# Preparing a graph-attention layer beside the last strips of an attention layer: other engines compare and normalise, and one score row travels through DRAM

## The chip, the cores and the metric

The kernel runs on one core of a Trainium2 chip. The metric is the device time in microseconds of one execution; three runs of the kernel before gave 799.28, 801.04 and 801.62 us, median 801.04 us. The trace is from a further, profiled execution.

## The reference, cut to what matters

```python
def ref(x, adj, Wq, bq, Wk, bk, Wv, bv, W, a):        # x: 4096 x 128, adj: 4096 x 4096
    h = max(layernorm(x), 0)
    q, k, v = h @ Wq.T + bq, h @ Wk.T + bk, h @ Wv.T + bv
    s = where(adj > 0, q @ k.T / sqrt(128), NEG)
    x = x + elu(softmax(s) @ v)                         # first layer
    h = max(layernorm(x), 0)
    hw = h @ W
    s1, s2 = hw @ a[:128], hw @ a[128:]
    e = where(adj > 0, leaky_relu(s1[:, None] + s2[None, :], 0.01), NEG)
    return x + hw + softmax(e, axis=1) @ h              # second layer
```

In the second layer exp(leaky_relu(s1+s2)) takes one of two products of a row factor and a column factor, by the sign of s1+s2. So the kernel needs one bit for each pair (i, j), the sign of s1[i]+s2[j], cut with the mask bit, and two matmuls of such fp8 bit matrices with weighted rows of h.

## The kernel before, in words

A strip is 128 rows of the 4096; T = 32 strips, NC = 8 chunks (also called groups) of four. The program has three blocks, and a block ends when every engine has finished its part of it.

Block 1 (up to about 40 us) normalises x and makes q, k and v. Block 2 is the first layer, one period for each strip: TensorE makes scores (L998 to L1000), VectorE adds the mask (L811), ScalarE takes the exponential (L691), the weights are turned (L1009, L1025, DMA transposes L549) and multiplied with v (L1044, L1045), and GpSimd (POOL) prepares mask bytes (L592) and masks (L607) and the ELU (L623 to L626), with VectorE's batch-norm statistics (L846) of the new x behind it. Each engine's order is written out by hand in a function `period`, and `all_periods` runs it.

Beside and behind the last strips block 2 prepares the second layer, chunk by chunk. VectorE's `variance` and `inverse_root` (L856 to L874) give the mean and 1/std; GpSimd's `normalise` (L635) subtracts and scales chunks 0 to 6, VectorE (L954) chunk 7; TensorE's `turn_h` (L1098) turns a chunk, ScalarE's `hT_out` (L767) copies it out; `s_products` (L1105, L1109) makes the s1 and s2 columns, and the s1 row spread over all partitions by a matmul with `wa_rep`; ScalarE's `s_out_of` (L773 to L777) copies both out; VectorE's `weigh` (L883) makes weighted h, GpSimd's `split_words` (L644) cuts it in a high and a low half; `hw_product` (L1114) and `add_hw` (L327) add hW. The signs of the first group's four strips are made for 32 key tiles: strips 0 and 1 (EARLY) in block 2, for each chunk two tiles on ScalarE (`sign_bytes`, L297), one on VectorE and one on GpSimd (`compare_bytes`, L302). At its end VectorE finds the maxima over all rows (L963 to L983, with TensorE L1133 to L1136) and cuts strip 0's bits (L312, L316, L321).

On the SyncE (SP) queue stand, after the last three transposes of block 2's own low parts (L549), eight DMA transposes (`load_mask`, L308) which bring the mask words of groups 0 and 1.

Block 3 is the second layer. For strips 2 and 3 of group 0 (LATE) the signs are still to be made: VectorE does ten tiles, GpSimd 22 (`VECTOR_LATE = 10`). `cut(0, 0, 2)` waits until both are done. TensorE runs 64 matmuls (L1466) for each strip, waiting for `parts_ready` of that strip and for `sums_out` of the strip two before. ScalarE makes the signs of group g+1 while TensorE runs group g: 11, 11 and 10 tiles of all four strips, each lot followed by `copy_sums` (L1401) of one strip, and the group's `signs_ready` after the third lot. `cut` of group g+1 waits for it. SP stores results and loads masks of group g+2.

## Time and profile before

| what | value |
|---|---|
| median of three runs | 801.04 us (799.28 to 801.62) |
| the profiled execution's own time | 802.26 us |
| its span, first to last instruction | 800.5 us |
| TensorE busy | 731.8 us, 91% of the span |
| VectorE, ScalarE, GpSimd busy | 572.9, 547.7, 481.9 us |
| mean granted TensorE clock | 0.963 of 2.4 GHz |

The span splits in three: block 1 to about 40 us, block 2 to about 547 us, block 3 to the end. In a timeline row stand the start in us from the span's start, the time in us, engine, line, operation, tiles out<-in with their shape and the count merged in the row; in brackets is how long the engine sat idle before and what released it. An "SPq" row is the time that the queue's sequencer took to issue. GpSimd (POOL) shares with VectorE (DVE) the way to the on-chip memory, so the same instruction is seen with more than one duration.

### The profile page before, as it was taken

What the parts mean: (1) busy time and instruction counts of PE and PEld (TensorE: products, weight loads), DVE (VectorE), ACT (ScalarE), POOL (GpSimd) and SP (SyncE); (2) the same over time, 40 slices, a digit from 0 to 9 for tenths busy, and PEclk for the clock granted to TensorE, in tenths of its full rate; (3) what the DMA queues carried; (4) which work ended last, traced back from release to release, by engine and by line L of the source; (5) the groups of instructions that cost most, each with busy time, mean ns of one, the idle gap of its engine ahead of it and who ended that gap; (6) DMA issues with size and microseconds to landing.
All of it is one profiled execution on the core that took longest, in us unless ns stands there. A gap on an engine that the chain in (4) does not pass through costs nothing. (4 is left out here: it accounts for less than half of the span.)

```text
span 800.5 us, 18318 instructions
## 1 busy us (share of the span) xinstructions
PE 731.8 (91%) x6229; PEld 613.4 (77%) x6229; DVE 572.9 (72%) x1219; ACT 547.7 (68%) x1082; POOL 481.9 (60%) x375
## 2 busy tenths in 40 slices
PE   4975999999999999999999998649299999999996
PEld 2554888888888888888888877438288888888885
DVE  4847687878787878787878894597294775685572
ACT  5944678787878787878787866445548977977910
POOL 1068499999999999999999969997700000000000
PEclk9987999999999999999999999688699999999999
DMA  6059999999898988888988646700043434334100
GB/s 223 1 187 246 271 212 264 251 264 255 254 257 255 255 256 256 254 256 255 255 255 255 198 94 108 157 0 1 1 106 73 90 70 86 86 84 88 36 10 12
DMA packets 189323, 130.86 MB, mean 163 GB/s; under 512 B 170336, under 2 KB 176992, under 8 KB 181088
## 3 DMA queue, kind: packets, MB, share of 16 engines
q1 hardware_dynamic: 188544, 130.05, 60.4%
q8 instruction: 24, 0.39, 0.2%
q10 hardware_dynamic: 576, 0.26, 0.1%
q14 instruction: 19, 0.16, 0.1%
q0 software_dynamic: 160, 0.00, 0.0%
HBM read 69.47 MB, written 18.87 MB: 110 GB/s over the span
## 5 line engine op out<-in xcount | busy, mean ns | idle before, releaser
L811 DVE CUSTOM_DVE_ANT_0 scores<-ps_s,mask_both 128x1024 f32<-128x1024 f32 x128 | 155.7, 1217 | 27.9 <-POOL mask_both L607 17.5
L592 POOL TENSOR_SCALAR mask_bytes<-adj_both 128x2048 uint8<-128x2048 int32 x64 | 146.2, 2301 | 44.8 <-POOLq L80 40.0
L691 ACT ACTIVATE scores<-scores,neg_max 128x1024 f32<-128x1024 f32 x128 | 146.0, 1142 | 24.8 <-DVE neg_max L817 24.8
L830 DVE TENSOR_TENSOR low<-scores 128x1024 bf16<-128x1024 f32 x96 | 137.5, 1432 | 27.0 <-ACT scores L691 22.5
L607 POOL TENSOR_SCALAR mask_both<-mask_bytes 128x2048 bf16<-128x2048 uint8 x64 | 151.4, 2365 | 5.4 <-POOL mask_bytes L592 0.4
L1044 PE MATMUL spare<-v_parts,hiT 128*128 128x256 bf16 x768 | 141.5, 274 | 8.0 <-DMA lowT<-low 7.3
L705 ACT ACTIVATE hiT<-spare 128x512 bf16<-128x512 bf16 (+1 forms) x128 | 103.0, 805 | 58.2 <-PE spare L1025 55.6
L1045 PE MATMUL spare<-v_parts,lowT 128*128 128x128 bf16 x768 | 134.7, 220 | 0.0
L1466 PE MATMUL ps_x<-q_parts,over_k 128*128 128x258 bf16 x1024 | 117.0, 275 | 15.4 <-DVE over_k L321 14.0
L1466 PEld LDWEIGHTS ps_x<-q_parts,over_k 128*128 128x128 fp8e4 x1024 | 99.5, 98 | 31.1 <-DVE over_k L321 14.3
L998 PE MATMUL ps_s<-k_hi,q_strip 128*128 128x512 f32 x256 | 113.9, 445 | 6.6 <-DVE row_max L811 4.3
L1000 PE MATMUL ps_s<-k_hi,q_strip 128*128 128x512 f32 x256 | 102.7, 401 | 0.0
L999 PE MATMUL ps_s<-k_lo,q_strip 128*128 128x512 f32 x256 | 102.0, 399 | 0.0
L1044 PEld LDWEIGHTS spare<-v_parts,hiT 128*128 128x128 bf16 x768 | 75.5, 98 | 16.5 <-issue 8.0
L297 ACT ACTIVATE v_parts<-s_block,s_col 128x512 fp8e4<-128x512 f32 x128 | 79.6, 716 | 0.0
L1401 ACT ACTIVATE sums<-ps_x,ac 128x258 f32<-128x258 f32 x64 | 26.5, 466 | 77.6 <-PE ps_x L1466 77.6
L1045 PEld LDWEIGHTS spare<-v_parts,lowT 128*128 128x128 bf16 x768 | 75.5, 98 | 0.7
L823 DVE TENSOR_TENSOR pT_low<-spare,pT_high 128x512 bf16<-128x512 f32 x64 | 44.0, 687 | 29.6 <-ACT pT_high L698 29.5
L1025 PE MATMUL spare<-ident_half,scores 128*128 128x128 bf16 x768 | 64.8, 220 | 0.0
L1025 PEld LDWEIGHTS spare<-ident_half,scores 128*128 128x128 bf16 x768 | 44.9, 98 | 25.5 <-issue 25.1
L698 ACT ACTIVATE pT_high<-spare 128x512 bf16<-128x512 f32 x64 | 37.7, 590 | 38.4 <-PE spare L1009 37.5
L998 PEld LDWEIGHTS ps_s<-k_hi,q_strip 128*128 128x128 f32 x256 | 49.4, 193 | 15.4 <-DVE row_max L811 5.1
(154 smaller groups left out, 1346.1 us busy)
## 6 DMA issues: line engine op xcount, KB each, us to landing
adj_both<-in_adj SPq DMA_DIRECT2D x64, 1024.0 KB, 5.3
mask_bytes_dram<-mask_bytes SPq DMA_DIRECT2D x32, 512.0 KB, 2.8
x_sb<-in_x SPq DMA_DIRECT2D x8, 256.0 KB, 7.8
out<-res SPq DMA_DIRECT2D x32, 64.0 KB, 1.5
lowT<-low SPq DMA_TRANSPOSE x96, 4.7
over_k<-mask_bytes_dram SPq DMA_TRANSPOSE x16, 4.5
scores<-mask_bytes_dram SPq DMA_TRANSPOSE x16, 4.6
raw_w<-in_L_gnn_Wq ACTq DMA_DIRECT2D x1, 64.0 KB, 3.1
```

The lines of the kernel that those rows point to most:

```text
L592: nc.gpsimd.tensor_scalar(mask_bytes[b % 2][:, half(h)], adj_sb[h], 1.0, 0.0, ALU.min, ALU.max).then_inc(bytes_ready, 1)
L607: nc.gpsimd.tensor_scalar(out, src, -NEG, NEG, ALU.mult, ALU.add).then_inc(mask_ready, 1)
L691: nc.scalar.activation(sc, sc, ACT.Exp, bias=neg_max[:, bn:bn + 1], accum_out=row_sum[:, bn, k:k + 1]).then_inc(exp_done, 1)
L705: nc.scalar.activation(hiT[k][:, half_of], ps_t[(2 + u) % 3][:].bitcast(BF16)[:, half_of], ACT.Copy).then_inc(hiT_ready, 1)
L811: nc.vector.tensor_tensor_reduce(out=scores[bn % 2][:, part(k)], in0=ps_s[k % 2][:], in1=mask[bn % 2][:, part(k)], scale=1.0, scalar=LOWES ...
L830: nc.vector.tensor_tensor(low[k][:], p, high_half(p), ALU.subtract).then_inc(low_done, 1)
L998: nc.tensor.matmul(o, high, k_hi[:, col], start=True, stop=False)
L1000: last = nc.tensor.matmul(o, rest, k_hi[:, col], start=False, stop=True)
L1025: last = nc.tensor.transpose(out[:, D * t:D * t + D], high[:, D * t:D * t + D], ident_half[:])
L1044: nc.tensor.matmul(ps_a[:], high, v_parts[:, t, :, :], start=(i == 0 and n == 0), stop=False)
L1045: last = nc.tensor.matmul(ps_a[:, 0, :], rest, v_parts[:, t, 0, :], start=False, stop=(i == NC - 1 and n == 3))
L1466: last = nc.tensor.matmul(ps_x[b % 2][k][:], by_key_tile(m, t)[:, b], v1[k][:, t, :].bitcast(BF16), start=(t == 0), stop=(t == T - 1))
```

## The change

- GpSimd's `normalise` and VectorE's use `(x + minus_mean) * rstd` in place of `(x - mean) * rstd`; VectorE makes `minus_mean`.
- VectorE normalises chunks 0 and 1 (at the start of its last period) and 7, GpSimd chunks 2 to 6. Statistics of chunks 0 to 6 are worked out in one go in the period of strip T-2, not in two lots in those of T-4 and T-2 (with the root of the first in T-3).
- GpSimd makes no sign bytes. Per chunk ScalarE makes three early tiles, VectorE one. Of the late ones VectorE makes 16, ScalarE 16 at its start of block 3, and ScalarE's lots for group 1 become 0, 16 and 16.
- The s1 row isn't made by TensorE and copied out by ScalarE; SP writes the s1 column of a chunk to DRAM (element by element) and reads it back spread over 128 partitions, in three pieces (chunk 0; 1 to 3; 4 to 7), behind the eight mask transposes in its queue.
- The order on TensorE, ScalarE, VectorE and GpSimd behind the last period is written anew: the ELU of the last strip comes before chunks 2 and 3 are copied out, all `hw_product` come before the maxima are turned, `cut(0, 0, 2)` comes before `add_last_hw`.

```diff
@@ sync, behind the last period
                     for b in range(4):
                         load_mask(sp, 1, b, 1)
+                    for i, cs in enumerate(S1_CHUNKS):          # 0:1, 1:4, 4:8
+                        sp.wait_ge(s_out, cs.stop)
+                        for c in range(cs.start, cs.stop):
+                            sp.dma_start(s1_dram[c].rearrange("t p -> p t"), s_col[:, 4 * c:4 * c + 4, 0],
+                                         allow_slow_non_contiguous=True).then_inc(s1_stored[i], 16)
+                        sp.wait_ge(s1_stored[i], 16 * (cs.stop - cs.start))
+                        row = s1_dram[cs.start:cs.stop].rearrange("c t p -> (c t p)")
+                        sp.dma_start(s1_row[:, 512 * cs.start:512 * cs.stop], row.partition_broadcast(D)).then_inc(s1_in[i], 16)
@@ gpsimd
-                            last = nc.gpsimd.tensor_scalar(h_sb[:, t, :], x_sb[:, t, :], stats["moments"][:, t, 0:1],
-                                                           stats["rstd"][:, t:t + 1], ALU.subtract, ALU.mult)
+                            last = nc.gpsimd.tensor_scalar(h_sb[:, t, :], x_sb[:, t, :], minus_mean[:, t:t + 1],
+                                                           stats["rstd"][:, t:t + 1], ALU.add, ALU.mult)
...
-                            for n in range(6):
+                            for n in range(BY_VECTOR, BY_VECTOR + 2):
                                 normalise(n)
                     all_periods(pool, period)
+                    normalise(5)
+                    add_elu(T - 2)
+                    normalise(6)
+                    add_halves(T - 1)
                     split_words(0)
-                    add_elu(T - 2)
-                    split_words(1)
-                    add_halves(T - 1)
-                    split_words(2)
                     add_elu(T - 1)
-                    for c in range(3):
-                        early_sign(c)
-                    for c in range(3, NC):
-                        early_sign(c)
+                    for c in range(1, NC):
                         split_words(c)
@@ scalar
-                        act.wait_ge(s1_made, c + 1)
-                        nc.scalar.activation(s1_row[:, 512 * c:512 * c + 512], ps_s1, ACT.Copy).then_inc(s1_out, 1)
                     def early_signs(c):
                         act.wait_ge(s_out, c + 1)
-                        act.wait_ge(s1_out, 1)
-                        for t in (4 * c, 4 * c + 1):
+                        act.wait_ge(s1_in[0], 16)
+                        for t in range(4 * c, 4 * c + 3):
...
+                    s_out_of(0)
+                    acc_copy(T - 1, 3)
+                    s_out_of(1)
+                    elu_exp(T - 1)
                     hT_out(2)
                     hT_out(3)
+                    for c in range(2, NC - 2):
                         s_out_of(c)
                         early_signs(c - 2)
+                        if c + 2 < NC - 1:
+                            hT_out(c + 2)
@@ vector
+                        if not ahead:
+                            for n in range(BY_VECTOR):
+                                normalise(n)
                         turned_low(s, 0)
                         low_part(s, b, 1)
...
                     weigh(0)
-                    early_sign(0)
-                    weigh(1)
-                    early_sign(1)
                     dve.wait_ge(epi_done, T - 1)
                     moments_of(T - 2)
-                    weigh(2)
-                    early_sign(2)
-                    weigh(3)
+                    aggregate(slice(T - 4, T - 1))
+                    weigh(1)
+                    early_sign(0)                     # waits for s1_in[0]
                     dve.wait_ge(epi_done, T)
                     moments_of(T - 1)
-                    variance(slice(28, 32))
+                    aggregate(slice(T - 1, T))
+                    add_eps(slice(28, 32))
                     inverse_root(slice(28, 32))
+                    normalise(NC - 1)
+                    early_sign(1)
+                    for c in range(2, NC - 1):
                         weigh(c)
                         early_sign(c)
-                        add_hw(c - 4)
+                        if c >= 3:
+                            add_hw(c - 3)
@@ block 3
-                VECTOR_LATE = 10
+                VECTOR_LATE = 16
-                @block.gpsimd
-                def _(pool):
-                    for t in range(VECTOR_LATE, T):
-                        last = compare_bytes(nc.gpsimd, 0, s1_row, t, LATE)
-                    last.then_inc(late_signs, 1)
@@ vector
-                        last.then_inc(late_signs, 1)
+                        last.then_inc(vector_late, 1)
+                        cut(0, 0, 2)
                         add_last_hw(dve)
-                        for b in range(2, 4):
-                            cut(0, 0, b)
+                        cut(0, 0, 3)
@@ scalar
+                        for t in range(VECTOR_LATE, T):
+                            last = sign_bytes(0, s1_row, t, LATE)
+                        last.then_inc(late_signs, 1)
...
-                                    for t in range(11 * b, min(11 * b + 11, T)):
-                                        last = sign_bytes(1 - par, s1_block[:], t)
+                                    first_group = isinstance(g, int) and g == 0
+                                    for t in (range(16 * b - 16, 16 * b) if first_group else range(11 * b, 11 * b + 11)):
+                                        if 0 <= t < T:
+                                            last = sign_bytes(1 - par, s1_block[:], t)
```

## Rows read from the trace of the kernel before

**Rows 1.** The chain that ended last, its last part: start us, us, what.
```profile
786.80 7.19 PE ps_x L1466 x64
```

**Rows 2.** The timeline of TensorE before and at the start of block 3.
```profile
529.88 1.10 PE L1109 MATMUL ps_s<-scores,wa_rep 128*128 128x512 f32 x2
...
540.91 6.29 PE L1114 MATMUL spare<-w_next,scores 128*128 128x128 f32 x32
548.56 14.47 PE L1466 MATMUL ps_x<-q_parts,over_k 128*128 128x258 bf16 x128 [1.36 <-issue]
577.07 15.97 PE L1466 MATMUL ps_x<-q_parts,over_k 128*128 128x258 bf16 x128 [14.03 <-DVE over_k L321]
```

**Rows 3.** The timeline of VectorE in block 3.
```profile
552.70 4.02 DVE L302 TENSOR_SCALAR over_k<-mask_both,s_col 128x256 uint8<-128x256 f32 x10
574.53 1.23 DVE L316 SCALAR_TENSOR_TENSOR over_k<-over_k 128x1024 uint32<-128x1024 uint32 x1 [14.82 <-POOL over_k L302]
```

**Rows 4.** By stretch: length, busy PE, PEld, DVE, ACT, POOL; granted clock; DMA.
```profile
532.00:534.00 2.00, 0.00 (x0) 0.00 (x0) 2.00 (x3) 2.00 (x6) 2.00 (x2) 0.61 0.00 0
580.00:582.00 2.00, 2.00 (x19) 1.69 (x17) 1.83 (x9) 0.00 (x0) 0.00 (x0) 0.95 0.00 0
```

**Rows 5.** The timeline of ScalarE, end of block 2 and start of block 3.
```profile
531.51 2.49 ACT L297 ACTIVATE over_k<-mask_both,s_col 128x256 fp8e4<-128x256 f32 x6
549.83 0.63 ACT L1409 ACTIVATE s_block<-mask_both 128x512 f32<-128x512 f32 x1
557.34 0.82 ACT L1401 ACTIVATE sums<-ps_x,ac 128x258 f32<-128x258 f32 x2
558.05 6.84 ACT L297 ACTIVATE v_parts<-s_block,s_col 128x512 fp8e4<-128x512 f32 x11
```

**Rows 6.** The waits of TensorE from 440 to 486 us.
```profile
PE spare L1044 <- DVE pT_low L823: 1.6, 1, 1.6
```

**Rows 7.** The timeline of VectorE beside the last strips and at block 2's end.
```profile
490.24 1.21 DVE L830 TENSOR_TENSOR low<-scores 128x1024 bf16<-128x1024 f32 x1
518.36 0.29 DVE L846 BATCH_NORM_STATS2 bn<-x_sb 128x6 f32<-128x128 f32 x1 [0.35 <-POOL x_sb L626]
519.94 0.17 DVE L868 TENSOR_SCALAR seed<-moments 128x4 int32<-128x4 int32 x1
522.38 2.59 DVE L954 TENSOR_SCALAR adj_both<-x_sb,moments,rstd 128x128 f32<-128x128 f32 x4
534.88 0.15 DVE L963 TENSOR_REDUCE hT_total<-hT_sum 128x1 f32<-128x8 f32 x1
543.38 0.68 DVE L327 TENSOR_TENSOR x_sb<-x_sb,spare 128x512 f32<-128x512 f32 x1
```

**Rows 8.** Single lines and tiles: ns min/median/max, first and last start.
```profile
L954 DVE TENSOR_SCALAR adj_both<-x_sb,moments,rstd x4: 340/786/1084, 522.4 to 523.9; 128x128 f32<-128x128 f32 x4
L302 DVE TENSOR_SCALAR over_k<-mask_both,s_col x18: 343/518/594, 502.8 to 556.2; 128x256 uint8<-128x256 f32 x18
L635 POOL TENSOR_SCALAR adj_both<-x_sb,moments,rstd x28: 785/787/1745, 478.1 to 504.3; 128x128 f32<-128x128 f32 x28
```

**Rows 9.** The timeline of the SP queue behind the last strip.
```profile
492.96 10.03 SPq L308 DMA_TRANSPOSE over_k<-mask_bytes_dram  x4
503.11 10.06 SPq L308 DMA_TRANSPOSE scores<-mask_bytes_dram  x4
```

**Rows 10.** DMA issues of the page, and of the first 25 us: KB, us to landing.
```profile
adj_both<-in_adj SPq DMA_DIRECT2D x64, 1024.0 KB, 5.3
out<-res SPq DMA_DIRECT2D x32, 64.0 KB, 1.5
...
scores<-mask_bytes_dram SPq DMA_TRANSPOSE x16, 4.6
...
a_cols<-in_L_gnn_a POOLq DMA_DIRECT2D x2, 0.5 KB, 7.0
```

**Rows 11.** Groups of instructions by line, 485 to 548 us: busy us, mean ns.
```profile
L883 DVE SCALAR_TENSOR_TENSOR q_parts<-adj_both,q_parts 128x512 f32<-128x512 f32 x16 | 16.3, 1060 | 7.0 <-ACT s_col L775 7.0
```

More of the change, by code:

```diff
@@ L285, in build @@
             sem("signs_ready"), sem("mask_scaled"), sem("lower_part_ready"), sem("mask_cut"))
-        late_signs, hw_made = sem("late_signs"), sem("hw_made")
+        late_signs, vector_late, hw_made = sem("late_signs"), sem("vector_late_signs"), sem("hw_made")
+        s1_in = [sem(f"s1_rows_in{i}") for i in range(3)]
         def by_key_tile(m, t, dt=FP8):
@@ L497, in build @@
                 turned_x = [ps_s[0][:, 512 * i:512 * i + 512] for i in range(2)]
-                ps_s2, ps_s1 = ps_s[1][:, 0:512], ps_s[1][:, 512:1024]
+                ps_s3 = [ps_s[1][:, 512 * i:512 * i + 512] for i in range(2)]
+                ps_s2 = ps_s3[0]
                 block = c2.enter_context(nc.Block())
@@ L848, in _, with aggregate, add_eps @@
                     tail = Steps(dve, tail_own)
+                    def aggregate(cs):
+                        dve.wait_ge(bn_done, cs.stop)
+                        for t in range(cs.start, cs.stop):
+                            tail.mark(nc.vector.bn_aggr(stats["moments"][:, t, :], stats["bn"][:, t, :]))
+                    def add_eps(cs):
+                        mean, var = stats["moments"][:, cs, 0], stats["moments"][:, cs, 1]
+                        tail.wait()
+                        tail.mark(nc.vector.tensor_scalar(minus_mean[:, cs], mean, -1.0, None, ALU.mult))
+                        tail.do(nc.vector.tensor_scalar(var, var, EPS, None, ALU.add))
                     def variance(cs):
-                        bn, moments, spread = stats["bn"][:, cs], stats["moments"][:, cs], newton[:, 0, cs]
+                        bn, moments, spread = stats["bn"][:, cs], stats["moments"][:, cs], newton[:, cs]
                         mean_e, mean_o, m2_e, m2_o = (bn[:, :, i] for i in (1, 4, 2, 5))
@@ L860, in variance @@
                                                                  in1=stats["root"][:, cs], op0=ALU.mult, op1=ALU.mult))
-                        tail.mark(nc.vector.tensor_scalar(mean, mean, 0.5, None, ALU.mult))
+                        tail.mark(nc.vector.tensor_scalar(minus_mean[:, cs], mean, -0.5, None, ALU.mult))
                         tail.do(nc.vector.tensor_scalar(var, var, 1.0 / D, EPS, ALU.mult, ALU.add))
@@ L876, in inverse_root, with normalise @@
                             tail.do(ins)
+                    def normalise(c):
+                        for t in range(4 * c, 4 * c + 4):
+                            last = nc.vector.tensor_scalar(h_sb[:, t, :], x_sb[:, t, :], minus_mean[:, t:t + 1],
+                                                           stats["rstd"][:, t:t + 1], ALU.add, ALU.mult)
+                        last.then_inc(h_by_vector, 1)
                     def weigh(c):
@@ L985, in _ @@
                     cut_upper(0, 0).then_inc(parts_ready, 1)
-                    add_hw(3)
                 @block.tensor
@@ L1077, in period @@
                             make_scores(s + 2, b % 2, 0)
-                        if not ahead:
-                            s_products(0)
                         turn_high(s, b, 2)
@@ L1084, in period @@
                             make_scores(s + 2, b % 2, 1)
-                        if not ahead:
-                            turn_h(2)
                         turn_high(s, b, 3)
@@ L1121, in _ @@
                     s_products(1)
+                    turn_h(2)
                     turn_h(3)
@@ L1136, in _ @@
                     nc.tensor.matmul(ps_s2[:, 0:2], ones[0:2, :], top_diag[:], start=True, stop=True).then_inc(top_b, 1)
-                    for c in range(4, NC):
-                        hw_product(c)
         if True:
@@ L1332, in general @@
                         add_last_hw(dve)
+                        for rows in s1_in:
+                            dve.wait_ge(rows, 16)
                         dve.wait_ge(g_high, 1)
@@ L1405, in body @@
                             if more:
+                                if isinstance(g, int) and g < 2:
+                                    act.wait_ge(s1_in[g + 1], 16 * 1)
                                 act.wait_ge(signs_ready, g + 1)
```

98 lines of the change are left out of this document (42 added, 56 removed).

## The prediction, made before the changed kernel was run

> **What bounds the kernel now.** I read the chain that ended last first, backwards from the end. It is TensorE's L1466 without a break, 64 matmuls and 7.18 us for each strip, up to 793.99 us, and then 6.5 us of copying, adding and storing to 800.5 [rows 1]. So in block 3 only what delays TensorE counts. The timeline of TensorE shows the one hole: strips 0 and 1 run from 548.56 to 563.03 us, strip 2 starts at 577.07, after 14.03 us of waiting [rows 2]. VectorE's timeline says for whom: its cut of strip 2 waits 14.82 us for GpSimd's compare L302, and starts 0.04 us after the last of 22 compares has ended at 574.49; cutting takes 574.53 to 577.07, 2.54 us [rows 3]. Behind the hole the granted clock is 0.5, that is 1.2 GHz, for some 3 us before it returns to 2.4 GHz [rows 4]; strips 2 and 3 take 15.81 us (577.07 to 592.88) where 14.36 are due, so the hole costs 1.45 us more. Before block 3, TensorE ends block 2 with 32 matmuls at the low clock, to 547.20, and the block change takes 1.36 us [rows 2]. I call the start of strip 0 T0, 548.56 before. Then the old end is T0 + 251.9.
>
> **Block 3 after the change.** VectorE's ten late compares took 4.02 us; 16 take 6.4 [rows 3]. From T0 + 4.1 (552.70) they end at T0 + 10.6, scale and cut of strip 2 (0.6 + 2.54) at T0 + 13.75, before strips 0 and 1 are done at T0 + 14.5. ScalarE's 16 late signs at 0.415 us (2.49 / 6) [rows 5] take 6.6 us from T0 + 1.3 to T0 + 7.9: hidden under VectorE's. So GpSimd's 14.03 us go. What is late next is ScalarE, which has taken over work and given up none. Its row copy and gate take 0.77 (549.83 to 550.60), a lot of eleven signs 6.73 from its start to the next copy (so 0.612 each) and the copy of one strip's sums 0.71 (557.34 to 558.05) [rows 5]. T0 + 7.9 + 0.77 + 0.71 + 16 x 0.612 + 0.71 + 16 x 0.612 = T0 + 29.7; only then are group 1's signs ready, VectorE cuts for 2.54 and strip 4 can start at T0 + 32.2. Strips 0 to 3 are done at T0 + 28.9, or T0 + 30.3 if strip 0 meets the low clock: a hole of 1.9 to 3.3 us takes the place of 14. The clock paid at T0 hides in it. The other 28 strips take 28 x 7.18 = 201.0, the tail 6.5: the end is T0 + 239.8, and block 3 gives 12.1 us. `add_last_hw` is moved behind the cut, 2.5 us before strip 3's cut, which is needed only at T0 + 21.7: free. For later groups ScalarE needs 32 x 0.612 + 4 x 0.71 + 0.77 = 23.2 us against 28.7 of TensorE: it catches up in group 2.
>
> **T0 after the change.** Three things move it.
>
> First, statistics. TensorE waits 1.6 us for VectorE once between 440 and 486 us [rows 6], beside the first statistics lot; that lot leaves, so all behind comes 1.6 us earlier. It returns in the period of T-2 as one lot 28 wide, with ops hardly longer than those 4 wide: nothing more.
>
> Second, VectorE's last period has eight `normalise` instructions ahead of its low parts. Four such took 2.59 us beside a busy GpSimd; the shortest single one took 0.34 us [rows 7, 8], and 0.27 apart is my estimate from it. So 2.2 to 5.2 us (GpSimd normalises at the same time, which speaks for the upper end). The last low part, done at 491.45 before [rows 7], is then done at 491 to 494. On it hang the last own transpose and, in one queue, the eight mask transposes, which are issued from 492.96 to 513.17 [rows 9]. They now end at 512.8 to 515.7; I take 514.3.
>
> Third, the row. Chunk 0's store stands behind them all, though its s1 column is made near 499. VectorE's `early_sign(0)` waits for it, and behind that wait stand the last strip's statistics, `normalise` of chunk 7, six `weigh` and the maxima; ScalarE's `early_signs(0)` waits too, with every later copy behind it. No row shows this store. The transposes before it land 2.1 us after their issue has ended (4.6 less 2.5), a 64 KB store lands in 1.5 us; the column loads of 128 single elements took 7.0 us from another, busy queue [rows 10]. The store has 512 elements: from 1.5 to 4 x 7.0 = 28 us. I take 2.8, since the 64 KB store is of the same queue and the column loads sat among the x loads. The read back of 256 KB lies between 1.5 (64 KB) and 5.3 (1 MB) [rows 10]; I take 2.4. With 0.2 for the waits the row is there 5.4 us after the queue is free: X = 519.7. [...]
>
> VectorE from X to the end of block 2, each between uncontended and contended with GpSimd: eight early compares 0.27 to 0.5 each; last statistics, about 0.9 ahead of a root of 2.44 (519.94 to 522.38); four `normalise` 1.1 to 2.6; six `weigh` (two instructions of 1.06 each on the mean, 16.3 for all eight) 1.3 to 2.1; four `add_hw` 0.6; maxima, turning, cuts 534.88 to 543.4, of which its own `weigh` and compare are counted already, some 5 to 6 [rows 7, 8, 11]. Sum 22 to 31. GpSimd now has only eight splits there and no compares, so I take 27.3. TensorE and ScalarE are done before: ScalarE's signs need about X + 16. With 1.35 for the block change T0 = 519.7 + 27.3 + 1.35 = 548.4, where it was 548.56. What leaves VectorE's path there (waiting for GpSimd's chain, which ended at 518.3 and now ends near 509) is eaten by the wait for the row; five early pieces of VectorE's work now stand behind it. TensorE's last 32 matmuls (6.29 us) go from the end to where it waits anyway: that is 3.1 us (547.20 against VectorE's 544.06) which the longer VectorE chain fills.
>
> **The sum.** 548.4 + 239.8 = 788.2 us of span against 800.5, 12.3 us less. The profiled execution took 802.26 us, 1.2 above the median of the runs; the median should fall by the same 12.3 to 788.7. GpSimd's `add` in place of `subtract` I count at nothing: its 20 `normalise` take at most 0.79 us each, 15.8 together [rows 8], from the statistics at about 483.5; with some 8 us of ELU, halves and one split the last ELU is done near 508 to 509, 10 us before X. Cheaper ones lengthen only that pause.
>
> **Rivals.**
> A, the forecast: the row at about 520, strip 4 late by ScalarE; 788.7. Chance 0.45.
> B, the lower bounds hold: VectorE is little disturbed and its work from X takes 23, T0 = 544; 784. For it, GpSimd drops 30 compares; against it, each `weigh` is followed at once by a split. Chance 0.18.
> C, the transfer is slower: 10 us from queue to row, T0 = 553, and the hole before strip 4 lets the clock fall (1.45 us); 795. After TensorE's instructions ended at 530.98 us the stretch from 532 to 534 has 0.61, so it fell near 532.4, 1.5 us into the pause [rows 2, 4]. Chance 0.21.
> D, slower than before: the store goes element by element at the price of the column loads, 28 us. Then X = 545, T0 = 574, the end 814. It decides from a round trip of 17.5 us (X = 532, T0 = 560.7). Against it, the low bound is a row of this very queue. Chance 0.09. The Trainium skill, DMA: Bandwidth & Descriptors, Rules for kernel authors, speaks against this change: a plain DMA with rearranged access is given as 19 times slower than the hardware transpose; 19 times 1.5 us would be that rival's 28 us. No row here shows it.
> E, no change: a round trip of 13 to 18 us, T0 near 560, gives back what block 3 gains; 801. Chance 0.07. That GpSimd's work merely moves, with ScalarE as late as GpSimd was, would need signs twice as long as measured; it is in this chance.
>
> **How the numbers follow.** The forecast is A, 789. Within 0.3% (2.4 us, about what this kernel's measurement can tell from no change) lies E; faster A, B and C, 0.84; slower D, 0.09. The range leaves out D, E and the edges of B: 782 to 798.
>
> **What would show it.** Right: no `L302` on GpSimd; no wait of VectorE for GpSimd in block 3; strip 4's matmuls preceded by 2 to 3 us of idle with ScalarE's signs before the cut; VectorE idle from about 504 to 520 before an L302 with a DMA as its releaser; the SP queue's mask transposes ended near 514 and the row 5 us later; strips at 7.18 us. Wrong: T0 beyond 553 or below 544; a hole before strip 2; VectorE's first idle put down to GpSimd; TensorE or ScalarE, not VectorE, ending block 2.

## The result and the profile after

The changed kernel takes 796.45 us, median of seven runs (794.48 to 798.74), beside 801.54 us for the kernel before in runs taken with them (799.28 to 803.25). The ratio is 0.9939, 95% interval 0.9919 to 0.9960: 5.1 us less, where 12.3 were forecast. The profiled execution took 797.06 us, its span is 795.3 us, 5.2 less than before.

| | before | forecast | after |
|---|---|---|---|
| row of chunk 0 in place (X) | | 519.7 | 524.8 |
| start of strip 0 (T0) | 548.56 | 548.4 | 553.95 |
| strip 2 starts | T0 + 28.5 | T0 + 14.5 | no hole |
| strip 4 starts | | T0 + 32.2 | T0 + 33.7 |
| end of the span | T0 + 251.9 | T0 + 239.8 | T0 + 241.35 |

The SP queue of the changed kernel, timeline (start us, us to issue, line, operation); it answers [rows 9]:

```profile
501.63 9.15 SPq L311 DMA_TRANSPOSE scores<-mask_bytes_dram  x4
510.83 0.58 SPq L587 DMA_DIRECT2D s_row_dram<-s_col  x1
521.25 0.33 SPq L591 DMA_DIRECT2D mask_both<-s_row_dram  x1
526.92 1.47 SPq L587 DMA_DIRECT2D s_row_dram<-s_col  x3
537.75 0.33 SPq L591 DMA_DIRECT2D mask_both<-s_row_dram  x1
541.17 2.01 SPq L587 DMA_DIRECT2D s_row_dram<-s_col  x4
552.13 0.33 SPq L591 DMA_DIRECT2D mask_both<-s_row_dram  x1
```

L587 stores the s1 column of one chunk, L591 reads the row back and can't be issued before the store is complete. The queue is free at 510.8. The read is issued 10.42 us after the store. The second piece, three stores, takes 10.83 us, the third, four stores, 10.96: in this execution the time hardly grows with the number of stores. Over the other runs with these waits three stores take 10.3 to 13.0 us and four 10.8 to 13.9. The view of the DMA queues from 508 to 522 us (40 slices of 0.35 us, tenths busy; then KB and us from issue to landing) shows when data moved:

```profile
DMA  9699999999999300000000000000000000000000
...
mask_both<-s_row_dram SPq DMA_DIRECT2D x1, 256.0 KB, 3.5
...
s_row_dram<-s_col SPq DMA_DIRECT2D x1, 2.0 KB, 10.4
```

The last data of the store and of the transposes ahead of it are through in the slice that ends at 513. Then the DMA engines show nothing for 8 us, until the store counts as landed.

The timeline of VectorE in its last period, at the wait for the row, at the end of block 2 and in block 3; it answers [rows 3, 7]:

```profile
484.09 2.13 DVE L898 TENSOR_SCALAR adj_both<-x_sb,minus_mean,rstd 128x128 f32<-128x128 f32 x8
...
524.77 0.36 DVE L305 TENSOR_SCALAR over_k<-mask_both,s_col 128x256 uint8<-128x256 f32 x1 [25.09 <-DMA mask_both<-s_row_dram]
...
550.67 1.22 DVE L324 TENSOR_TENSOR over_k<-over_k 128x1024 uint32<-128x1024 uint32 x1
553.93 0.24 DVE L1267 TENSOR_SCALAR z_top<-s_col,top 128x32 f32<-128x32 f32 x1 [2.03 <-issue]
...
557.76 4.29 DVE L305 TENSOR_SCALAR over_k<-mask_both,s_col 128x256 uint8<-128x256 f32 x16
```

VectorE stands still for 25.1 us, released by the DMA, then works without a pause to 551.89. SP's last read is issued at 552.13, a little later, and block 2 ends by that: strip 0 starts 1.82 us behind it (T0 = 553.95), as it does 1.8 to 1.9 us behind the last read in every run below that has this read in block 2. In block 3 VectorE waits for nobody before strip 2 (rows not shown). The 16 late compares take 4.29 us, 0.27 each.

TensorE at the same place, and ScalarE, which now makes signs where GpSimd compared [rows 2, 5]:

```profile
549.32 0.58 PE L1153 MATMUL ps_s<-top_diag,ones 2*128 2x2 f32 x2 [3.32 <-DVE top_diag L993]
553.95 31.41 PE L1484 MATMUL ps_x<-q_parts,over_k 128*128 128x258 bf16 x256 [4.05 <-issue]
587.67 3.75 PE L1484 MATMUL ps_x<-q_parts,scores 128*128 128x258 bf16 x32 [2.31 <-DVE scores L324]
```

```profile
555.05 6.50 ACT L300 ACTIVATE over_k<-mask_both,s_col 128x256 fp8e4<-128x256 f32 x16
...
563.94 0.84 ACT L1415 ACTIVATE sums<-ps_x,ac 128x258 f32<-128x258 f32 x2 [1.64 <-PE ps_x L1484]
564.67 9.91 ACT L300 ACTIVATE v_parts<-s_block,s_col 128x512 fp8e4<-128x512 f32 x16
574.47 0.83 ACT L1415 ACTIVATE sums<-ps_x,ac 128x258 f32<-128x258 f32 x2
575.19 9.91 ACT L300 ACTIVATE v_parts<-s_block,s_col 128x512 fp8e4<-128x512 f32 x16
```

Strips 0 to 3 run in one piece; the 14.03 us hole is gone. A hole of 2.31 us stands before strip 4, behind ScalarE's two lots of 16 signs for group 1 (L300, `v_parts`). Strips 0 to 3 take 31.41 us where 28.7 are due. The stretches of the windows view (length, busy PE, PEld, DVE, ACT, POOL; granted clock; DMA) say why [rows 4]:

```profile
550.00:552.00 2.00, 0.00 (x0) 0.00 (x0) 1.83 (x4) 0.00 (x0) 0.00 (x0) 0.50 0.00 0
...
556.00:558.00 2.00, 2.00 (x11) 1.36 (x10) 1.97 (x3) 2.00 (x6) 0.00 (x0) 0.50 0.35 147
558.00:560.00 2.00, 2.00 (x13) 1.51 (x12) 2.00 (x9) 2.00 (x6) 0.00 (x0) 0.64 0.00 0
560.00:562.00 2.00, 2.00 (x20) 1.74 (x19) 2.00 (x9) 2.00 (x5) 0.00 (x0) 1.00 0.03 8
```

TensorE meets strip 0 at a granted 0.5, that is 1.2 GHz, and works 11 matmuls in 2 us instead of 20 until about 559.4. From the end of the last `hw_product` at 545.24 to strip 0, 8.7 us, it had done five small matmuls.

### The profile page after: what moved, and what is told of

Same layout as the page of the kernel before. It is cut to its first block and busy times, and to the rows that moved or that the text cites. A ratio compares the mean times of both kernels' runs of the same rounds, so it can differ in the third digit from the quotient of the medians.

```text
span 795.3 us, 18259 instructions
## 1 busy us (share of the span) xinstructions
PE 725.0 (91%) x6213; PEld 612.1 (77%) x6213; DVE 564.8 (71%) x1213; ACT 553.2 (70%) x1098; POOL 431.8 (54%) x337
## 5 line engine op out<-in xcount | busy, mean ns | idle before, releaser
L1014 PE MATMUL ps_s<-k_hi,q_strip 128*128 128x512 f32 x256 | 112.8, 440 | 8.4 <-DVE row_max L816 6.1
L1016 PE MATMUL ps_s<-k_hi,q_strip 128*128 128x512 f32 x256 | 101.6, 397 | 0.0
L300 ACT ACTIVATE v_parts<-s_block,s_col 128x512 fp8e4<-128x512 f32 x128 | 79.6, 719 | 0.0
```

The costliest lines, as they stand in the source:

```text
L1014: nc.tensor.matmul(o, high, k_hi[:, col], start=True, stop=False)
L1016: last = nc.tensor.matmul(o, rest, k_hi[:, col], start=False, stop=True)
```

## The experiments

Each was timed beside the kernel before on the same chip; ratios are to that, and not all experiments ran on one chip. Times in rows are of one profiled execution each, which can lie some 3 us from the median of its kernel. "..." in a diff marks where lines are left out.

**1. Block 3 alone.** The kernel before with only the edits of block 3:

```diff
-                VECTOR_LATE = 10
+                VECTOR_LATE = 16
...
-                @block.gpsimd                      # 22 compares
...
+                        for t in range(VECTOR_LATE, T):      # scalar
+                            last = sign_bytes(0, s1_row, t, LATE)
...
-                                    for t in range(11 * b, min(11 * b + 11, T)):
+                                    for t in (range(16 * b - 16, 16 * b) if first_group else range(11 * b, 11 * b + 11)):
```

> The kernel before with only block 3's part of the change: 16 late tiles on VectorE, 16 on ScalarE, none on GpSimd, ScalarE's lots 0, 16, 16, cut of strip 2 ahead of the last additions. Theory S (the change's block 3 gives 11 to 12 us, and its preparation, through the late row, takes 5 to 7 us back): block 3 starts where it did, at 548.6 us, and ends 240 to 241 us later, so the span is 789 and the median about 789 us, faster than the whole change by 6 to 7 us. Rival L (ScalarE's late lots spoil most of the gain wherever block 3 starts): the hole before strip 4 is over 6 us and the time is that of the whole change, 795 us or more.

Measured 792.82 us (791.78 to 793.48) beside 800.25; ratio 0.9908 (0.9875 to 0.9942). TensorE's timeline:

```profile
543.79 5.91 PE L1114 MATMUL spare<-w_next,scores 128*128 128x128 f32 x32
551.07 28.78 PE L1465 MATMUL ps_x<-q_parts,over_k 128*128 128x258 bf16 x256 [1.37 <-issue]
583.09 5.00 PE L1465 MATMUL ps_x<-q_parts,scores 128*128 128x258 bf16 x32 [3.23 <-DVE scores L321]
```

The span is 790.9: T0 + 239.8, the forecast's own number. Strip 4 starts at T0 + 32.0, where 32.2 was forecast. Behind that two differences nearly cancel. The first half of strip 4 takes 5.00 us instead of 3.74, as the granted clock fell in the hole of 3.23 us (0.50 in the stretch from 583 to 585), which the sum didn't have; and from the last matmul to the end it is 5.4 us instead of 6.5. T0 is 2.5 us later than in the profile of before; VectorE is 2.2 us later already at 503, where nothing was changed, so that is one execution against another. By the medians block 3 gives 7.4 us (5 to 10 by the ratio's interval), by the two profiles 12.1 behind T0. The time lies between the expected 789 and the rival's 795; the hole, 3.23 us and not over 6, speaks for the first. This part alone does as well as the whole change or better: the parts in block 2 gain nothing in sum.

**2. Chunk 0's row by TensorE again.** The changed kernel, but the row of chunk 0 is one matmul with `wa_rep` and one copy by ScalarE, as before; the other seven chunks still go through DRAM.

```diff
+                        if c == 0:
+                            nc.tensor.matmul(ps_s3[1], wa_rep[:], hT2[:, 0:512], ...).then_inc(row_made, 1)
...
+                        if c == 0:
+                            act.wait_ge(row_made, 1)
+                            nc.scalar.activation(s1_row[:, 0:512], ps_s3[1], ACT.Copy).then_inc(s1_in[0], 1)
...
-                        dve.wait_ge(s1_in[0], 16)
+                        dve.wait_ge(s1_in[0], 1)
```

> The changed kernel, with chunk 0 of the score row made as before the change (one matmul with the repeated column, one ScalarE copy) and only chunks 1 to 7 through DRAM. Theory S: VectorE's 25 us and ScalarE's 20 us of waiting for the row vanish, VectorE's 27 us of work from the last strip's statistics on starts at about 505 in place of 525; the SP queue's last store (wait for the last s1 column near 521, then 11 us) ends with it; block 3 starts at 533 to 537 and the time is 775 to 781 us. Rival V (VectorE was bound by its own work or by GpSimd's chain anyway and the wait only took up slack): block 3 starts later than 548 and the time stays above 790 us.

Measured 782.91 us (779.75 to 784.52), 2 us above what was expected; ratio 0.9793 (0.9757 to 0.9828). Against the changed kernel that is 13.5 us less by the medians and 11.7 by the ratios, each taken beside the kernel before. Its VectorE ends block 2 at 533.2 instead of 551.9; its SP queue and TensorE:

```profile
521.43 2.09 SPq L590 DMA_DIRECT2D s_row_dram<-s_col  x4
534.42 0.33 SPq L594 DMA_DIRECT2D mask_both<-s_row_dram  x1
```

```profile
536.28 30.37 PE L1494 MATMUL ps_x<-q_parts,over_k 128*128 128x258 bf16 x256 [5.07 <-issue]
```

The wait for one row cost more than the 7.1 us of span by which the forecast was missed. VectorE's path is 18.7 us shorter, T0 17.7: SP's last read is issued 1.2 us after VectorE is done, so the SP queue, waiting for its own last stores, sets the end of block 2. Chunks 4 to 7 of the row are needed only in block 3, but their wait stands in block 2. The hole before strip 4 is 2.31 us again, and here the first half of strip 4 takes 5.39 us behind it, against 3.75 in the changed kernel, so T0 + 241.7 is the end. Why the clock fell in one hole of this length and not in the other stays open.

**3. The store ahead of the transposes.** Chunk 0's store is issued before the eight mask transposes and its read between the two fours.

```diff
+                    sp.wait_ge(s_out, 1)
+                    sp.dma_start(s1_dram[0].rearrange("t p -> p t"), s_col[:, 0:4, 0], ...).then_inc(s1_stored[0], 16)
                     for b in range(4):
                         load_mask(sp, 0, b, 0)
+                    sp.wait_ge(s1_stored[0], 16)
+                    sp.dma_start(s1_row[:, 0:512], ...).then_inc(s1_in[0], 16)
```

> The changed kernel, with chunk 0's store issued ahead of the eight mask transposes in the SP queue and read back between the two fours. Theory S (the store itself takes 10 us from issue to landing wherever it stands): it lands near 506, the read back is issued near 507 and lands near 510, block 3 starts near 541 and the time is 781 to 786 us. Rival Q (the store is slow because transposes are in flight ahead of it): it lands 2 to 3 us after its issue at 496; the read back still waits its turn to 507, so the time is the same, and the landing time of the store tells the two apart.

Measured 794.86 us (791.17 to 797.75, ten runs); ratio 0.9925 (0.9904 to 0.9946): the changed kernel's 0.9939 within its interval. The SP queue:

```profile
494.17 0.39 SPq L579 DMA_DIRECT2D s_row_dram<-s_col  x1
494.60 18.69 SPq L311 DMA_TRANSPOSE over_k<-mask_bytes_dram  x4
513.34 0.58 SPq L584 DMA_DIRECT2D mask_both<-s_row_dram  x1
...
551.03 0.33 SPq L596 DMA_DIRECT2D mask_both<-s_row_dram  x1
```

The store took 11.2 us from issue to landing here too, ahead of all eight mask transposes, so its price is not the transposes ahead of it. But the four transposes behind it took 18.69 us to issue, where four take 9 to 10 elsewhere, and used up 9.4 of the 16.7 us by which the store was earlier: the row arrives at 517.5. In the view of the DMA queues the engines are all but idle from 499 to 504.5 and move 1 to 8 GB/s, though transposes are in flight; from about 505, when the store lands (505.4), they move 77 GB/s and more. So the transposes hardly went on while the store was unfinished; why, no run shows. VectorE is done with block 2 at 544.6, 7.3 us earlier, and T0 gains only 1.1 of it, since SP's last read is issued at 551.03 and T0 is 552.88. The expected 781 to 786 us didn't come: the store landed as expected, but neither the transposes' delay nor SP's end was in that sum.

**4. The same 2 KB in one piece.** TensorE makes chunk 0's row on one partition, ScalarE copies it there, SP stores 2 KB from one partition to 2 KB in a row; the read is unchanged.

```diff
+                        if i == 0:
+                            sp.wait_ge(row_out, 1)
+                            sp.dma_start(s1_dram[0:1].rearrange("c t p -> c (t p)"), one_row[:]).then_inc(s1_stored[0], 16)
```

> The changed kernel, with chunk 0's row made contiguous on one partition (a matmul with the single column, a ScalarE copy of 1 x 512) and stored from there in one piece of 2 KB, at the same place in the SP queue; the read back and chunks 1 to 7 are unchanged. Theory S, element form (it is the 4-byte elements that take 10 us to complete): the store lands in about 2 us, the row is there near 517 in place of 525, block 3 starts near 546 and the time is 787 to 790 us. Rival F (any small store to DRAM that is waited for takes 8 to 10 us to report, whatever its elements): nothing moves, 796 us.

Measured 787.49 us (786.64 to 791.32); ratio 0.9852 (0.9808 to 0.9896).

```profile
509.50 0.42 SPq L590 DMA_DIRECT2D s_row_dram<-one_row  x1
511.85 0.34 SPq L596 DMA_DIRECT2D mask_both<-s_row_dram  x1
```

Same queue, same place, same bytes: 2.35 us instead of 10.42, near the 2.8 that the prediction had taken. T0 is 545.19, and 9.0 us are won by the medians, 7.0 by the ratios. It was the form of the store, source and destination taken together. VectorE is done at 541.99, so SP's last read, issued at 543.34, sets T0 here too.

**5. Four forms of a store, one after the other.** Ahead of the contiguous store of experiment 4, SP stores 512 elements four times, each waited for: into one 2 KB row as the change does (`again_dram`), into elements 512 B apart (`pad_dram`), four side by side for each partition from `s_col`, whose elements lie 12 B apart (`lines_dram<-s_col`), and the same from a source with the four side by side (`lines_dram<-bv_rep`). One execution, 807.34 us, longer by what it adds.

```diff
...
+  forms = ((again_dram.rearrange("t p -> p t"), s_col[:, 0:4, 0]),
+           (pad_dram[:, :, 0].rearrange("t p -> p t"), s_col[:, 0:4, 0]),      # pad_dram: 4 x 128 x 128
+           (lines_dram[0], s_col[:, 0:4, 0]),                                  # lines_dram: 2 x 128 x 4
+           (lines_dram[1], bv_rep[:, 0:4]))
+  for n, (dst, src) in enumerate(forms):
+      sp.dma_start(dst, src, ...).then_inc(form_stored[n], 16)
+      sp.wait_ge(form_stored[n], 16)
```

> Measures stores to DRAM by themselves, one after the other in the SP queue behind the mask transposes, each waited for (the kernel is longer by them): 512 elements of 4 bytes into one contiguous row of 2 KB; the same 512 elements each 512 bytes from the next; the same 512, four of a partition side by side; 128 pieces of 16 bytes, four of a partition side by side; at last 2 KB from one partition in one row. Theory E (the element count or size sets the 10 us): the first three take about 10 us each, the 16-byte form 2 to 4. Theory C (writes from many engines into the same few lines of DRAM finish late): the first takes about 10, the second and third about 2 to 3 us.

```profile
510.25 0.53 SPq L599 DMA_DIRECT2D again_dram<-s_col  x1
519.44 0.36 SPq L599 DMA_DIRECT2D pad_dram<-s_col  x1
521.87 0.64 SPq L599 DMA_DIRECT2D lines_dram<-s_col  x1
528.63 0.34 SPq L599 DMA_DIRECT2D lines_dram<-bv_rep  x1
531.25 0.30 SPq L601 DMA_DIRECT2D s_row_dram<-one_row  x1
532.42 0.35 SPq L607 DMA_DIRECT2D mask_both<-s_row_dram  x1
```

From issue to the next issue: 9.2, 2.4, 6.8, 2.6 and 1.2 us. The padded form moves the same 512 single elements as the first in a quarter of its time, so neither the number of elements nor their source is the price by itself. The order isn't either: the first form took 9.2 to 11.2 us in four runs, at different places in the queue, the contiguous one 2.35 in its place in experiment 4. Of the two expected theories neither came out whole: by the first the padded form would have taken about 10 us, by the second the third form 2 to 3. What the slow two share, and the padded form lacks, is many 4-byte writes close to each other in DRAM; 16-byte writes side by side are fast again. The Trainium skill, DMA: Bandwidth & Descriptors, Specifications, says that below 512 B a DMA engine does read-modify-write. By itself that doesn't fit, as the padded writes are 4 B too and took 2.4 us. That such writes hold each other up when they meet in the same stretch of DRAM would fit all five numbers, but this is argued, from one execution; no run here shows what the memory does.

**6. ScalarE without late signs.** The changed kernel, VectorE makes 28 of the 32 late tiles, ScalarE four, and ScalarE's lots are 11, 11 and 10 again.

```diff
-                VECTOR_LATE = 16
+                VECTOR_LATE = 28
...
-                                    for t in (range(16 * b - 16, 16 * b) if first_group else range(11 * b, 11 * b + 11)):
+                                    for t in range(11 * b, min(11 * b + 11, T)):
```

> The changed kernel with 28 of the 32 late tiles on VectorE (0.27 us each in the changed kernel's trace) and 4 on ScalarE (0.40 each), and ScalarE's lots of group 1 again 11, 11 and 10. Theory S: ScalarE's lots are the cause of the new hole of 2.3 us before strip 4; with them back the hole goes, VectorE's cut of strip 2 is ready at T0 + 14.6 us, before strips 0 and 1 (slow clock) are done at T0 + 17, so the span is 2.3 us shorter and the time 794 us. Rival W (the hole only hides what is late anyway, the cut of strip 2 or the slow clock): strip 2 or 4 still waits over 1.5 us and the time stays 796.

Measured 792.57 us (791.53 to 793.74); ratio 0.9891 (0.9863 to 0.9919), on another chip than the changed kernel's 0.9939.

```profile
552.33 30.97 PE L1482 MATMUL ps_x<-q_parts,over_k 128*128 128x258 bf16 x256 [4.14 <-issue]
583.14 3.74 PE L1482 MATMUL ps_x<-q_parts,scores 128*128 128x258 bf16 x32
```

No hole before strip 4, and the span ends at T0 + 237.9 instead of T0 + 241.35; the 28 compares take 7.44 us, 0.27 each, and VectorE's cut of strip 2 is still in time. That the new hole is ScalarE's chain of late signs and lots is shown. How much of it is the 12 signs fewer and how much the lot of 11 that now stands ahead of the first copy of sums, the run doesn't separate.

**7. GpSimd subtracts again.** The kernel of experiment 2, with the mean subtracted as before; once on another chip than experiment 2, and then as a pair on one chip.

```diff
-  last = nc.gpsimd.tensor_scalar(h_sb[:, t, :], x_sb[:, t, :], minus_mean[:, t:t + 1], ..., ALU.add, ALU.mult)
+  last = nc.gpsimd.tensor_scalar(h_sb[:, t, :], x_sb[:, t, :], mean_of[:, t:t + 1], ..., ALU.subtract, ALU.mult)
```

> The kernel in which TensorE makes chunk 0's row, with GpSimd subtracting the mean again in its five chunks (VectorE makes one small multiplication more). Theory S2 (now that the wait for the row is gone, GpSimd's chain up to the last strip's ELU sets when VectorE may start its last 27 us, so its cost is paid in full): 20 instructions of 0.79 in place of about 0.43 us move the last ELU from 504.9 to about 511, block 3 starts 5 to 6 us later and the time is 787 to 789 against 782.9. Rival N (GpSimd's chain has slack there, or VectorE's sharing hides it): within 1.5 us of 782.9.

Measured 783.05 us (782.34 to 784.13), ratio 0.9766 (0.9740 to 0.9793), against 782.91 and 0.9793 for experiment 2 on another chip. The expected 787 to 789 didn't come, the rival's "within 1.5 us" did; so the pair followed.

> The kernel with chunk 0's row made by TensorE and ScalarE again, word for word, as the mark for the next run on the same chip: 779.8 to 784.5 us as before, most likely 782.5; strip 0 of the last block at 536 to 538 us; GpSimd's four tiles of add and multiply ahead of the last chunk 1.7 us.

> The same, but GpSimd subtracts the mean again instead of adding its negative (one more small VectorE operation of 128x8 per chunk makes the mean). Theory S, the subtraction is what makes GpSimd's normalise slow and the last chunk's chain of ELUs ends with it: the four tiles take 3.1 us instead of 1.7, the last ELU ends 4 to 6 us later than in the run above, strip 0 starts 4 to 5 us later, time 4 us (0.5%) above the run above. Theory N, GpSimd's normalise is not what the end of the block hangs on: within 1.5 us of the run above.

Adding: 783.56 us (780.57 to 785.02), ratio 0.9775 (0.9752 to 0.9797). Subtracting: 785.58 (783.07 to 787.04), ratio 0.9791 (0.9768 to 0.9815). The medians are 2.0 us apart, the intervals overlap. GpSimd's rows, adding and then subtracting:

```profile
490.70 1.75 POOL L651 TENSOR_SCALAR adj_both<-x_sb,minus_mean,rstd 128x128 f32<-128x128 f32 x4
...
504.24 0.46 POOL L642 TENSOR_TENSOR x_sb<-x_sb,att_exp 128x128 f32<-128x128 f32 x1
```

```profile
494.44 3.13 POOL L652 TENSOR_SCALAR adj_both<-x_sb,mean_of,rstd 128x128 f32<-128x128 f32 x4
...
511.70 0.45 POOL L643 TENSOR_TENSOR x_sb<-x_sb,att_exp 128x128 f32<-128x128 f32 x1
```

0.44 against 0.78 us for a tile of 128x128, and the last ELU 7.5 us later (1.5 of it stands already before GpSimd's first tile, one execution against another). VectorE is then done with block 2 at 540.1 instead of 532.6. T0 moves by only 4.2 (539.23 to 543.47), as block 2 is held by SP's last read in both, issued at 537.40 and 541.65. The expected 4 us lie in the profiles; but the subtracting one, 787.04 us, is the slowest of its five runs. The medians show half, and with the first run, where they show nothing, a gain is not safely apart from none.

**8. All together.** Experiment 2, with the wait for the last stores and their read moved to SP's part of block 3, 28 late tiles on VectorE, and the last ELU on GpSimd ahead of the first split.

```diff
@@ sync, block 2
+                        if i == 2:
+                            continue
                         sp.wait_ge(s1_stored[i], 16 * (cs.stop - cs.start))
...
@@ gpsimd
-                    split_words(0)
                     add_elu(T - 1)
-                    for c in range(1, NC):
+                    for c in range(NC):
@@ sync, block 3
+                    sp.wait_ge(s1_stored[2], 16 * 4)
+                    sp.dma_start(s1_row[:, 2048:], ...).then_inc(s1_in[2], 16)
```

> A version meant to be faster than both: TensorE makes chunk 0's row, the wait for the last store and its read back stand at the start of block 3, the lots are 11, 11, 10 with 28 late tiles on VectorE, and GpSimd does the last ELU ahead of its first split. Theory S: block 2 ended 1.5 us after VectorE for the SP queue's store, the hole before strip 4 was 2.3 us, the ELU comes 2 us earlier: block 3 starts near 532.5, the span is 770 to 773 us and the time 774 to 778. Rival B (block 2's end is bound elsewhere, by ScalarE's or TensorE's chunks, once the store is gone): block 3 starts at 535 or later and the time is 779 or more.

Measured 772.63 us (771.68 to 774.49); ratio 0.9641 (0.9617 to 0.9665). This is 3.6% faster than the kernel before and, by the two ratios, some 3% faster than the changed one.

```profile
523.98 2.08 SPq L590 DMA_DIRECT2D s_row_dram<-s_col  x4
537.45 0.33 SPq L1230 DMA_DIRECT2D mask_both<-s_row_dram  x1
```

```profile
535.32 30.96 PE L1496 MATMUL ps_x<-q_parts,over_k 128*128 128x258 bf16 x256 [3.38 <-issue]
566.12 3.74 PE L1496 MATMUL ps_x<-q_parts,scores 128*128 128x258 bf16 x32
```

The last read is issued 2 us after strip 0 has started, and VectorE's end of block 2 (533.95) sets T0 again, 1.37 us later. T0 = 535.32 is not the expected 532.5 and lies where the rival put it, though the time lies below both. The ELU ahead of the split brought little: GpSimd waits 0.82 us for ScalarE there, and VectorE is no earlier than in experiment 2 (533.2). What was won lies in the SP wait and behind T0: the end is T0 + 237.4, against T0 + 241.7 in experiment 2. Experiment 9 timed this kernel again beside that of experiment 2 (`row0_by_pe_b`) on one chip: 774.56 against 783.56 us.

**9. Work for TensorE nearer to strip 0.** The combined kernel, with the products of chunks 6 and 7 behind the turning of the maxima, beside the combined kernel again.

```diff
-                    hw_product(NC - 2)
-                    hw_product(NC - 1)
...
+                    # behind the matmul that turns the maxima
+                    hw_product(NC - 2)
...
+                    # behind the matmul that spreads them
+                    hw_product(NC - 1)
```

> The combined kernel again, as the mark for the next run on the same chip: 772.6 us (771.7 to 774.5), strip 0 at 535.3 us, strips 0 to 3 in 31.0 us with a granted clock at half at their start.

> The combined kernel with its last two products of h and the weights put behind the last chunk's transposes of the scores, so that TensorE has work nearer to strip 0. Theory H, the clock fell because TensorE had too little to do ahead of strip 0, and these products keep it up: strips 0 to 3 take 28.8 to 29.5 us instead of 31.0, the granted clock in the first 5 us of strip 0 is above 0.9, time 1.5 to 2.2 us below the run above. Rival, the products are too short to keep it up, or what waits for them now ends later: strips 0 to 3 still take 30.5 to 31 us, or strip 0 starts 0.5 to 1.5 us later, and the time is the same or up to 1.5 us longer.

The combined kernel again: 774.56 us (773.48 to 775.99), ratio 0.9661 (0.9641 to 0.9681). With the products moved: 773.69 us over six runs, five from 770.81 to 777.12 with a median of 772.52 and one of 1511.14 that nothing here explains; ratio without that one 0.9651 (0.9620 to 0.9682). The ratios don't tell the two apart. What the products should have done, the profile decides; the moved ones of chunk 7 and strips 0 to 3:

```profile
529.60 2.08 PE L1137 MATMUL spare<-w_next,scores 128*128 128x128 f32 x8
533.04 31.29 PE L1496 MATMUL ps_x<-q_parts,over_k 128*128 128x258 bf16 x256 [1.36 <-issue]
```

```profile
535.00:537.00 2.00, 2.00 (x11) 1.42 (x10) 1.97 (x3) 1.97 (x6) 0.00 (x0) 0.50 0.70 258
537.00:539.00 2.00, 2.00 (x14) 1.51 (x13) 2.00 (x9) 2.00 (x5) 0.00 (x0) 0.67 0.68 274
```

The products run at the low clock themselves, and strips 0 to 3 take 31.29 us as they take 31.34 without. Here 1.91 and 2.08 us of matmuls with pauses between did not bring the clock back; the 2.3 to 2.5 us there are still lost. In the kernel before 6.3 us of them without a pause, ended 1.36 us ahead of strip 0, stood at this place: the granted clock came back in them (0.98 in the stretch from 546 to 548), and strips 0 and 1 ran at full speed [rows 2]. Experiment 1 kept them there (5.91 us) and took 28.78 us for four strips. These are the only two kernels without the low clock at T0; a run that puts nothing but this piece back into the changed kernel was not made.

## Why the prediction was right or wrong

The sign was right, and 796.45 lies in the range, but the gain was 5.1 us and not 12.3. On the spans, 795.3 stands against a forecast of 788.2; the 7.1 us between them, term by term:

| term | forecast | measured | difference |
|---|---|---|---|
| SP queue free for the store | 514.3 | 510.8 | -3.5 |
| store of chunk 0 | 2.8 | 10.42 | +7.6 |
| read back, with the waits | 2.6 | 3.52 | +0.9 |
| VectorE from X to its end | 27.3 | 27.12 | -0.2 |
| block change | 1.35 | 2.06 | +0.7 |
| from T0 to the end | 239.8 | 241.35 | +1.55 |

**The step that failed** is the store's 2.8 us. It was taken from a store of 64 KB in long runs, on the ground that it was of the same queue, between bounds of 1.5 and 28; the row nearest in form was the other one, the column loads of single elements, and what differed between the two rows was not the queue. 10.4 us is well inside the bounds. The contiguous store measured the term the sum had: 2.35 us, and the time was 787.5 beside the forecast's 788.7. That the two times are so near is in part luck: T0 was 545.19 and not 548.4, since the queue was free earlier, and the end T0 + 241.3 and not T0 + 239.8. Rival C, a slow transfer, is what happened to the row: it gave X = 524, T0 = 553 and 795, at a chance of 0.21. Its clock term didn't come as it was put, a fall in the hole before strip 4: behind that hole the granted clock is 1.00 and the first half of strip 4 takes 3.75 us. The low clock stood at T0 instead. T0 = 553.95 is beyond the 553 that the prediction itself had put under "wrong".

**Rival D**, the store at 28 us, didn't come true: it took 10.42 us, 4.4 times the contiguous one of the same bytes (2.35). The factor of 19 that stood beside it, from the Trainium skill, DMA: Bandwidth & Descriptors, Rules for kernel authors, is between a rearranged plain DMA and the hardware transpose; no run here measured that pair, and 19 times 1.5 us was not the store's price. That four stores in flight took hardly longer than one (10.96 to 10.42 us in the changed kernel) also speaks against a price for each element.

**The clock at T0.** The forecast put it as hidden in the hole before strip 4, since ScalarE's chain was thought to start from its own work. It doesn't hide: `copy_sums` of strip 0 waits until strip 0 is done, at T0 + 9.97 instead of T0 + 7.18, and ScalarE, ready at T0 + 8.3, stood 1.64 us for it. Behind that copy stand both lots of 16, so strip 4 came at T0 + 33.7 instead of 32.2. That is the +1.55. The low clock itself comes with a move that the forecast counted as free: TensorE's last 32 products, read there as run at the low clock to 547.20, had the granted clock back from about 546 on, ahead of strip 0 (experiment 9 says how far it is shown that the move cost it).

**The block change.** The forecast named SP's queue for the row's start, not for the end: that the wait for the third piece's stores stands in block 2, and so ends it, wasn't in the sum. Strip 0 starts 1.8 to 1.9 us behind SP's last read in every kernel with that read in block 2, and 1.37 us behind VectorE in the combined one without it. The wait costs 0.7 us here, and 1.7 to 6.9 where VectorE was faster (experiments 2, 3, 4 and the adding kernel of 7).

**What was right.** Block 3's gain and its mechanism: T0 + 28.8 for four strips in experiment 1, strip 4 at T0 + 32.0, the new hole before it and its cause (experiment 6); that the end came out at T0 + 239.8 exactly is in part luck, as said there. VectorE idle until a DMA releases it, with five pieces of its work behind. VectorE's 27.3 us from there, measured 27.12, though it was a pick from between 22 and 31 that no term singled out. The eight `normalise` on VectorE took 2.13 us, the lower end of 2.2 to 5.2. With that and the statistics lot gone the SP queue was free 3.5 us before the value taken; as experiment 1 shows a shift of 2.2 us between two executions of the same instructions, no more is read into it. GpSimd's `add`, counted at nothing, was worth nothing in this kernel: the last ELU was done 20 us before the row. With the row early it lies on VectorE's chain (experiment 7, by the profiles; the medians don't settle what it is worth), and the reason given, that at most 0.79 us each still fits ahead of X, holds only while X is late.

## What to carry to other kernels

A small store has a form before it has a size: where a transfer's price must come from other rows, take the row nearest in form, with pieces of the same length at the same distance at the destination, and keep a bound for the time between the last data and the completion. Here that time was 8 of 10.4 us. An engine that only waits for a transfer can end a block; put a wait where its result is needed, and ask of each wait in an in-order queue what stands behind it, as one row of 2 KB held 27 us of VectorE's work here. When a hole is filled by moving work to an engine that gives nothing up, find that engine's next due date, and put its waits for other engines into the sum.

## What the runs showed of the hardware

- A single store of 512 elements of 4 B into one 2 KB stretch of DRAM completed in 9.2 to 11.2 us (four runs); in the changed kernel the last data on the queues were through some 2 us after its issue. With the elements 512 B apart it took 2.4 us, in 16 B runs 2.6 from a source with the four side by side and 6.8 from one with them 12 B apart (one execution each), in one piece 1.2 and 2.35.
- Four DMA transposes issued behind such a store took 18.7 us instead of 9 to 10 (one execution).
- Strip 0 of block 3 starts 1.37 us after VectorE's last instruction of block 2 in the combined kernel, and 1.8 to 1.9 us after SP's last read where that read ends block 2.
- The same hole of 2.3 us before strip 4 left the clock up in the changed kernel (first half of strip 4 in 3.75 us) and down in experiment 2 (5.39 us).
- GpSimd's `tensor_scalar` on 128x128 fp32 takes 0.44 us with add and multiply, 0.78 with subtract and multiply, each in a row of four; single ones beside a busy VectorE took up to 1.5 and 1.9 us.
- VectorE's compare of 128x256 took 0.27 us each in a row of 16 with GpSimd idle, 0.40 in the row of ten before, with GpSimd comparing beside it.
